# A recurrence on one NeuronCore: the history product with its operands exchanged, and its result returned through DRAM

## The reference

```python
def step(St, inp):                     # St: [channels i, keys j]
    kt, qt, vt, at, bt = inp
    err = einsum('bhij,bhj->bhi', St, kt) - vt
    Sn = at[..., None] * St - (bt[..., None] * err)[..., None] * kt[:, :, None, :]
    return Sn, einsum('bhij,bhj->bhi', Sn, qt)
```

## Time and profile before

| | us |
|---|---|
| median of 3 runs (range) | 3216.29 (3214.12 to 3221.67) |
| the profiled execution: its time | 3229.24 |
| the same: its span | 3227.6 |
| mean granted TensorE clock | 0.823 |

### The profile page before, as it was taken

The page is one execution under the profiler, slowest core; times in us unless marked ns, Lnnn a source line. Parts: engine busy times, 40 slices in busy tenths (PEclk is TensorE's granted clock), DMA queues, the critical chain, the costliest instruction groups (busy, mean ns, idle before and its releaser), DMA issues. The chain is left out here.

```text
span 3227.6 us, 46717 instructions
## 1 busy us (share of the span) xinstructions
PE 2577.4 (80%) x13906; PEld 2056.3 (64%) x13906; DVE 2220.5 (69%) x5854; ACT 1249.3 (39%) x2980; POOL 773.3 (24%) x700
## 2 busy tenths in 40 slices
PE   8999999993899999898989888859987572279900
PEld 5666666663788888888888788757862251147700
DVE  5777777769888889998999988855636656013334
ACT  2555555544355555554555444713320010012200
POOL 1333333331000000000000000024435225601166
PEclk8999999997687878876878778889998765579955
DMA  2333333331223355565667768043312231029833
GB/s 68 118 107 114 117 107 114 117 114 56 73 73 102 102 132 131 150 155 161 170 179 203 201 184 234 20 147 90 89 55 70 85 145 67 12 66 265 251 94 91
DMA packets 488859, 389.68 MB, mean 121 GB/s; under 512 B 146239, under 2 KB 423534, under 8 KB 484472
## 3 DMA queue, kind: packets, MB, share of 16 engines
q1 hardware_dynamic: 440283, 283.52, 31.4%
q0 software_dynamic: 27936, 89.45, 9.0%
q10 hardware_dynamic: 20480, 14.69, 1.4%
HBM read 215.39 MB, written 178.41 MB: 122 GB/s over the span
## 5 line engine op out<-in xcount | busy, mean ns | idle before, releaser
L553 DVE SCALAR_TENSOR_TENSOR p_zo<-p_w,p_gd,p_zo 128x128 f32<-128x128 f32 x2304 | 649.2, 346 | 11.6 <-DVE p_zo L550 0.5
L819 PE MATMUL p_ps_z<-p_gcol,p_turned 112*128 112x32 f32 x3584 | 572.0, 324 | 53.8 <-DMA p_turned<-history 40.7
L819 PEld LDWEIGHTS p_ps_z<-p_gcol,p_turned 112*128 112x128 f32 x3584 | 566.2, 249 | 62.5 <-issue 37.8
L378 DVE SCALAR_TENSOR_TENSOR p_y<-p_ps_proj,p_w,p_y 128x508 f32<-128x508 f32 (+2 forms) x576 | 415.9, 741 | 111.8 <-ACT p_y L292 98.2
L798 PE MATMUL p_ps_x<-p_w,p_diag_o 128*128 128x128 f32 x2048 | 315.0, 305 | 68.8 <-ACT p_diag_o L860 47.2
L229 PE MATMUL p_ps_proj<-p_x,p_w 128*128 128x512 f32 x768 | 341.8, 595 | 2.7 <-ACT p_beta_t L283 2.7
L860 ACT ACTIVATE p_diag_o<-p_ident,p_gd 128x128 f32<-128x128 f32 x1024 | 316.2, 389 | 64.5 <-PE p_ps_x L798 55.6
L798 PEld LDWEIGHTS p_ps_x<-p_w,p_diag_o 128*128 128x128 f32 x2048 | 273.4, 209 | 105.9 <-ACT p_diag_o L860 65.8
L873 ACT ACTIVATE p_diag_z<-p_ident,p_gd 128x128 f32<-128x128 f32 x768 | 247.1, 390 | 208.2 <-PE p_ps_x L777 185.3
L777 PE MATMUL p_ps_x<-p_w,p_diag_z 128*128 128x128 f32 x1536 | 258.4, 316 | 60.9 <-DVEq L572 43.5
L777 PEld LDWEIGHTS p_ps_x<-p_w,p_diag_z 128*128 128x128 f32 x1536 | 220.3, 219 | 73.3 <-issue 49.3
(11 more groups left out here) (213 smaller groups left out, 3686.9 us busy)
## 6 DMA issues: line engine op xcount, KB each, us to landing
history<-p_hist SPq DMA_DIRECT2D x18, 2048.0 KB, 11.1
gram<-p_gram SPq DMA_DIRECT2D x64, 512.0 KB, 3.2
p_wgu<-in_wguT SPq DMA_DIRECT2D x64, 352.0 KB
decays<-p_dec SPq DMA_DIRECT2D x64, 256.0 KB, 2.3
beta_v<-p_bv SPq DMA_DIRECT2D x64, 256.0 KB, 2.4
p_dec<-decays POOLq DMA_DIRECT2D x32, 512.0 KB, 6.4
p_w<-beta_v POOLq DMA_DIRECT2D x16, 1024.0 KB, 6.1
heads_out<-p_zo POOLq DMA_DIRECT2D x16, 1024.0 KB, 9.4
```

Of the source, the lines that this page charges most:

```text
L378: nc.vector.scalar_tensor_tensor(out=yv[:, :, s:], in0=pv[:, :, 0:T - s], scalar=par[j][:, kind, TAPS - 1 - s:TAPS - s], in1=yv[:, :, s:], ...
L553: return done(nc.vector.scalar_tensor_tensor(out=acc, in0=row, scalar=scalar, in1=acc, op0=ALU.mult, op1=ALU.add))
L819: last = nc.tensor.matmul(ps_z[k % 2][:, u % UB * HU + h, :], turned[i][:, h, :], gcol[i][:, h, :], start=True, stop=True)
```

## The change

The operands of the history product change places. The 32 gram columns are stationary, and the four heads of a unit take partitions 0 to 31, 32 to 63, 64 to 95 and 96 to 127 of the output, so four column groups of the array; the 128 channels of the updates move. A batch (4 units, one sequence) fills one PSUM bank [128, 4, 128], of four such banks (two before). The result has its gram columns in partitions already. ACT copies each batch to `sums` and issues the DMA that writes it to a DRAM tensor `history_sums`; SP reads it back into `zo[g]` in two halves of 64 partitions, after all unit loads of the leaf. The transposes, `z_turn` and ACT's copies to `zo` are gone. `ORDER` is gone too: `cross_o` has no units between its steps, then come 24 units in one piece, then `cross_z` with the remaining eight.

```diff
-    ORDER = ((0, 3, 12, 10, 4), (3, ROUNDS, 14, 8, 5))
+    FIRST = 24
+    NZ = 4
-        z_turn = m.sb("p2_z_turn", [DH, P, 2 * C])
+        sums = m.sb("p2_sums", [P, BG, UB, DH])
-        ps_z = [m.ps(f"p2_ps_z{i}", [DH, H, 2 * C]) for i in range(2)]
-        ps_t = [m.ps(f"p2_ps_t{i}", [P, 4, DH]) for i in range(2)]
+        ps_z = [m.ps(f"p2_ps_z{i}", [P, UB, DH]) for i in range(NZ)]
@@ vector
-                dve.wait_ge(zo_ready[g], c + FREE)
+                if c:
+                    dve.wait_ge(zo_in[g], c * (2 * DMA))
@@ sync, after the 32 units of a leaf
+                    sp.wait_ge(o_out[g], (c + 1) * DMA)
+                    if c + 1 < ROUNDS:
+                        sp.wait_ge(kept[g], (c + 1) * 2)
+                    for half in range(2):
+                        seqs = slice(half * ZB * H, (half + 1) * ZB * H)
+                        sp.wait_ge(z_out[half], (c * GR + g + 1) * ZB * DMA)
+                        sp.dma_start(zo[g][seqs].rearrange("p f s i -> p (f s) i"), sums_dram[g, seqs]).then_inc(zo_in[g], DMA)
@@ tensor
-                                last = nc.tensor.matmul(ps_z[k % 2][:, u % UB * HU + h, :], turned[i][:, h, :],
-                                                        gcol[i][:, h, :], start=True, stop=True)
+                            last = nc.tensor.matmul(ps_z[k % NZ][h * 2 * C:(h + 1) * 2 * C, u % UB, :], gcol[i][:, h, :],
+                                                    turned[i][:, h, :], start=True, stop=True)
-                        cross_o(c, g, history_past(o_units))
-                        for _ in range(min(first, len(todo))):
-                            history(todo.pop(0))
-                        cross_z(*following(c, g), history_past(z_units))
-                        for u in todo:
-                            history(u)
...
+                    cross_o(c, g)
+                    for _ in range(FIRST):
+                        history(todo.pop(0))
+                    cross_z(*following(c, g), history_past(4))
@@ scalar
-                nc.scalar.copy(z_turn[:, b * H:(b + 1) * H, :], ps_z[k % 2][:]).then_inc(z_cp, 1)
+                if at and b % ZB == 0:
+                    act.wait_ge(z_out[b // ZB], at * ZB * DMA)
+                nc.scalar.copy(sums[:, b], ps_z[k % NZ][:]).then_inc(z_cp, 1)
+                act.wait_ge(z_cp, c * (GR * BG) + k + 1 + NZ)
+                act.dma_start(sums_dram[g, b * H:(b + 1) * H].rearrange("(q h) e i -> (h e) q i", h=HU),
+                              sums[:, b]).then_inc(z_out[b // ZB], DMA)
-                rows_after = (2, 2, 2, 8, 12, 16, 16, 16) if c < 3 else (2, 2, 9, 13, 16, 16, 16, 16)
+                rows_after = (2, 2, 2, 2, 2, 2, 9, 13)
...
```

More of the change, by code:

```diff
@@ L408, in projections, with recurrence @@
     clear(nc, used)
-def recurrence(nc, a_dram, bv_dram, gram_dram, beta_dram, hist_dram, o_dram):
+def recurrence(nc, a_dram, bv_dram, gram_dram, beta_dram, hist_dram, sums_dram, o_dram):
     GR = 2
@@ L494, in recurrence @@
         z_cp = m.sem("p2_z_cp")
-        t_done = m.sem("p2_t_done")
-        t_cp = m.sem("p2_t_cp")
-        zo_ready = [m.sem(f"p2_zo_ready{g}") for g in range(GR)]
+        z_out = [m.sem(f"p2_z_out{half}") for half in range(2)]
+        zo_in = [m.sem(f"p2_zo_in{g}") for g in range(GR)]
         TD = 2
-        TB = 2 * C // 4
+        ZB = BG // 2
         FREE = 1
@@ L505, in _ @@
             def _(sp):
-                for sem in (*zo_ready, mm_done, z_cp, t_done, t_cp):
-                    sp.sem_inc(sem, FREE)
+                sp.sem_inc(mm_done, FREE)
+                sp.sem_inc(z_cp, NZ)
                 sp.sem_inc(diag_o_used, NDO)
@@ L727, in _ @@
                 pool.wait_ge(o_out[g], DMA * NCHUNK)
+            for half in range(2):
+                pool.wait_ge(z_out[half], GR * ROUNDS * ZB * DMA)
         @block.sync
@@ L806, in _ @@
             cross_z(0, 0)
[L807 to L818, removed]
-                                last = nc.tensor.matmul(ps_z[k % 2][:, u % UB * HU + h, :], turned[i][:, h, :],
-                                                        gcol[i][:, h, :], start=True, stop=True)
[L821 to L827, removed]
-                                    history(todo.pop(0))
-                            return between
-                        cross_o(c, g, history_past(o_units))
-                        for _ in range(min(first, len(todo))):
-                            history(todo.pop(0))
-                        cross_z(*following(c, g), history_past(z_units))
-                        for u in todo:
-                            history(u)
[L837 to L843, removed]
@@ new lines, in _, with history, history_past, between @@
+            with pe.Fori(0, ROUNDS) as c:
+                for g in range(GR):
+                    def history(u):
+                        n = g * UNITS + u
+                        i = n % NTURN
+                        k = g * BG + u // UB
+                        pe.wait_ge(turned_in[i], c * (GR * UNITS // NTURN * TD * DMA) + (n // NTURN + 1) * TD * DMA)
+                        pe.wait_ge(z_cp, c * (GR * BG) + k + 1)
+                        for h in range(HU):
+                            last = nc.tensor.matmul(ps_z[k % NZ][h * 2 * C:(h + 1) * 2 * C, u % UB, :], gcol[i][:, h, :],
+                                                    turned[i][:, h, :], start=True, stop=True)
+                        last.then_inc(mm_done, 1)
+                    todo = list(range(UNITS))
+                    def history_past(units):
+                        def between(u):
+                            if todo and u > units:
+                                history(todo.pop(0))
+                        return between
+                    cross_o(c, g)
+                    for _ in range(FIRST):
+                        history(todo.pop(0))
+                    cross_z(*following(c, g), history_past(4))
+                    assert not todo
@@ L904, in _ @@
                     assert not todo
[L905 to L912, removed]
             diagonals_o(NCHUNK - 1, 0)
@@ L1916, in decoder_layer @@
     projections(nc, i["xT"], i["w_heads"], i["ba"], i["wbT"], i["bb_col"], i["bb_row"], a, bv, gram, beta)
-    recurrence(nc, a, bv, gram, beta, hist, o)
+    recurrence(nc, a, bv, gram, beta, hist, scratch("history_sums", 2, P, 2 * C, DH), o)
     attention_out(nc, i["x"], i["xT"], o, i["wgT"], i["woT"], i["ln_g"], i["ln_b"], x1, x1T)
```

3 lines of the change are left out of this document (1 added, 2 removed).

## The result

| | before | after |
|---|---|---|
| median (range), same chip | 3215.98 (3214.12 to 3221.67) | 3318.84 (3308.21 to 3325.96) |
| ratio after to before | | 1.0314, 95% interval 1.0278 to 1.0350 |
| the profiled execution: time | 3229.24 | 3313.03 |
| the same: span | 3227.6 | 3311.4 |
| mean granted TensorE clock | 0.823 | 0.799 |

A forecast was written before the change was run, and what follows sets the result against it. DVE's waits, 116.2 us, bound what could be won. First fills 58.7 and later fills 19, in two leaves a round, made 155 us, so +39: 3268 profiled, 3255 median; the case's own range 3214 to 3286.

The forecast's parts named there:

- D: The end of a leaf, from which the prediction counts its times; 1744.6 in the profiled leaf of round 5 before the change.
- F: Time from D to SP's first turned load: 8.1 to 28.4 us over rounds 0 to 6, plus a shift of 1.5 or 3.
- the 55 that I gave as my bound: Sign on PE: the prediction is wrong if `cross_z` starts before D+55 in round 5.
- the later fills: DVE's waits for `cross_z` after a leaf's first fill: 1, 1.5, 2.5, then 3.5 us a leaf, 19 over seven rounds.
- X: Time for 24 units' loads, the longer of SP's issue (22.9 us) and DMA work; 24.4 to 35.4 in rounds 3 to 6.
- the third fill's four steps: Reason for later waits of 3.5 us where DVE is ahead: the third fill is held by four diagonal steps.
- ACT's last copy: Reason for later waits: the copy and a DMA issue, about 0.5 us, stand ahead of the third diagonal, holding the second fill.
- The gate: 24 units ahead of `cross_z` put the first fill at D + F + X + 6.9; waits 0 to 21.7 us, together 58.7.
- the tail: Part after X, before `cross_z`: landing 2.6 us and one cold unit 0.9; with 3.4 to DVE's take, 6.9.
- PE per unit: History unit on PE in four column groups takes half of today's time, 0.45 us hot and 0.9 cold.
- Rival (b): On PE nothing overlaps and the clock stays low: a unit costs 1.72 us, waits 375, +259, time 3475; chance 0.10.
- DMA work of rounds 5 and 6: DMA engines' work in X: 22.3 and 25.9 us for units, plus 9.5 for sums' stores, decays and output store.

## Why the prediction was wrong, and where it was right

**Right.** The direction, and the mechanism. DVE's own work is fixed and only its waits count. PE's busy time is no measure: it fell by 374 us while the kernel lost 103. `cross_z` is gated by the landing of 24 units in late rounds. The returned sums make nobody wait in the changed kernel. `w`'s load goes out 7.9 us after D, and F moved by 2.6 to 4.5 us in rounds 3 to 6. In round 5 `cross_z` starts at D+60.1, above the 55 that I gave as my bound. What failed are sizes in the sum, two above all: the later fills, and X in round 3.

**The first step that failed: "The later fills".** Forecast 38, measured 64.0, +26: the largest single term. I took them at 1 to 2.5 us a leaf where DVE was not ahead. But DVE already waited for the first fill in rounds 0 to 2 (0.2 to 8.5 us), and the later ones cost 3.9 to 4.8 in each of these leaves: 17 of the 26 us. The other 9 are rounds 3 to 6, where my 3.5 was 1.2 low. Before's own timeline argued against me, with 5.3 to 6.3 us at later fills in each leaf of rounds 0 to 2. Of my two reasons, the third fill's four steps held; ACT's last copy did not. I also priced a diagonal step at 0.75 us, and without a unit it takes 1.00 behind ACT's diagonals.

**The second: "The gate", X in round 3.** I took "24 x 0.95" for SP's issue in all rounds, from one leaf of round 5, and 24.4 us of DMA work above it in round 3. SP's issue there is 24 x 1.33 = 31.9 us, with the DMA engines at 0.78. First fills waited 33.9 us in place of 11.8, 11 us more in each of the two leaves. Of these 11, X is 8.6 (33.0 us from the first turned issue to the 24th), F 1.5 and the tail 1.4, less 0.3 from `cross_z` to the take. So X in round 3 is 17 us of the miss. The kernel with the rows moved shows that it goes with the 64 partitions.

**PE per unit.** Taken 0.45 hot and 0.9 cold, measured 0.35 and at most 0.66. For the first fills the size did not matter, as I said: even 1.00 left them at 130.6 us. For the later fills it does. There I had 0.75 + 0.45 = 1.2 for a step and a unit, and it is 0.87 + 0.35 = 1.22, so two errors cancelled by luck. Why a step takes 0.12 longer beside a unit in column groups (0.87 with one group too) is not shown. The Trainium skill's "TensorE: Matmul & The Clock Gate", Part 3, lets weight loads overlap only across row groups; here all of a unit's operands share their rows, and four column groups still made a unit 2.8 times faster. So the Trainium skill's "TensorEngine Tiling (Array Packing)", When to Use Tiling, was the page to follow. Rival (b) is out. That the two records of one head can't overlap, my reason for 0.45, was not tried.

**The tail.** From the 24th turned issue to `cross_z` I had 2.6 + 0.9 = 3.5 us; after has 3.6 to 5.9. The 2.6 was the landing in a stretch at 58.8% of the DMA engines. In the stretch of round 5 that now sets the gate, 1829 to 1856, all queues together take 100%, and loads land in 4.6 us:

```profile
q1 hardware_dynamic: 10637, 5.19, 73.1%
q0 software_dynamic: 416, 1.57, 16.8%
q10 hardware_dynamic: 1584, 0.79, 9.8%
...
p_turned<-history SPq DMA_DIRECT2D x23, 192.0 KB, 4.6
```

The small waits of rounds 0 and 1 are tail too, since the 24th load goes out within 1 us of the forecast there in three leaves of four. But in round 0 the tail is longest (5.8 and 5.9) although the median load lands in 2.8 us, so the landing does not explain it there, and the cause stays open. Round 2's second leaf (8.5 us) has another reason: F there is 18.4, 3.6 above before's 14.8, where I took 1.5.

**DMA work of rounds 5 and 6 was too high.** The same rows give 27 us of work for what I priced at 31.8: three batches of sums moved (0.79 MB), not five, and a unit cost 0.73 x 27 / 23 = 0.86, not 0.93. So first fills in rounds 5 and 6 waited 14 us less than forecast, which by luck hid part of the miss.

**The account.** 133.8 - 117.4 = +16.4 and 64.0 - 38 = +26.0: 42.4 of waits, against 45 between the forecast (3268) and the profiled execution (3313). The other 19 of the 64 us between 3255 and the median 3318.8 come from 13 + 6, by which the two profiled executions lie on opposite sides of their medians. I had carried before's 13 over to after, which nothing supported.

**Left open.** Why SP's issue takes longer for 64 partitions than for 48 or 80 is not shown by any run. That POOL's earlier loads are what moved F is argued from their place among the stores; no run leaves them out. The share of the tail in the waits of round 2 was not tried by itself.

## What to carry to other kernels

Where one engine's fixed work sets a stage, list its waits and ask what stands ahead of each in the releasing engine's queue; the busy share of the engine that is made faster says nothing. When a change couples a faster operation with a new order, price each alone: here the operation, with its return, is worth -85 us and the order +188. Where a consumer waits several times in a row, read each of its waits apart: here the later ones were three quarters of the sum. Where a number is to hold for every round of a loop, read it in every round, for a size in the middle can be the dearest.

## What the runs showed of the hardware

- A load that puts 64 time steps in partitions keeps SP 0.61 to 0.63 us with its issue, one with 16, 32, 48, 80, 96 or 112 in partitions 0.42 to 0.49 (medians by round, SP's timeline of after). Seen in round 3 of before and after, and it moved with the size to round 4.
- Four fp32 matmuls (112 rows, 32 stationary columns, 128 moving) take 0.35 us in four column groups and 1.00 us in one, weight loads included, at the high clock. At the low clock, 0.50, the four groups are busy for at most 0.66 us.
- A diagonal step of six records over the full array and a unit in four column groups alternate at 1.22 us, 0.87 and 0.35, without an idle gap between them in PE's rows. Beside a unit of before, over all columns, the same step takes 0.75.
- A load of 192 KB lands in 2.6 us (median) where its queue takes 58.8% of the DMA engines, and in 4.6 us where all queues take 100%.
